# One list transfer per round of the attention loop instead of six

## What is computed

```python
xw = (x @ W).reshape(n_nodes, H, C)
al_s = einsum('nhc,hc->nh', xw, a_src);  al_d = einsum('nhc,hc->nh', xw, a_dst)
logits = leaky_relu(al_s[src] + al_d[dst], 0.2)
m = segment_max(logits, dst)
e = exp(logits - m[dst])
out = segment_sum((e / segment_sum(e, dst)[dst])[:, :, None] * xw[src], dst)
```

## Time and profile before

| what | us |
|---|---|
| median of three runs | 5478.3 |
| span of the profiled execution | 5521.1 |
| loop of layer 0 (from its first gather to its last) | 1356 |
| loop of layer 1 | 1364 |
| loop of layer 2 | 1346 |
| everything else | 1455 |

### The profile page before, as it was taken

The page is one execution under the profiler, slowest core; times in us unless marked ns, Lnnn a source line. Parts: engine busy times, 40 slices in busy tenths (PEclk is TensorE's granted clock), DMA queues, the critical chain, the costliest instruction groups (busy, mean ns, idle before and its releaser), DMA issues. The chain is left out here.

```text
span 5521.1 us, 62679 instructions
## 1 busy us (share of the span) xinstructions
PE 2641.6 (48%) x13804; PEld 1929.0 (35%) x13804; DVE 2377.2 (43%) x7341; ACT 594.6 (11%) x1968; POOL 2781.1 (50%) x2942
## 2 busy tenths in 40 slices
PE   1666774354444555557444554545543333333334
PEld 1555543123333333335233333333433323323323
DVE  5888513334444444442444444444423333333333
ACT  2222300110000000003000000000020000000001
POOL 2000011366666666663566666666446666666663
PEclk9766877667777767768677767677765555555555
DMA  2222564133333333341333333333313222222222
GB/s 61 106 106 96 233 217 157 26 86 89 88 91 88 90 88 91 88 87 44 80 90 89 88 89 92 88 90 90 69 33 46 46 47 46 46 47 46 47 45 22
DMA packets 246608, 451.11 MB, mean 82 GB/s; under 512 B 163452, under 2 KB 165314, under 8 KB 241709
## 3 DMA queue, kind: packets, MB, share of 16 engines
q0 software_dynamic: 122928, 318.15, 24.3%
q1 hardware_dynamic: 111150, 128.71, 6.9%
q10 hardware_dynamic: 12384, 2.25, 0.2%
HBM read 392.07 MB, written 57.21 MB: 81 GB/s over the span
## 5 line engine op out<-in xcount | busy, mean ns | idle before, releaser
L495 POOL DMA_INDIRECT rows_all<-gat_tab,ell x2664 | 2517.1, 945 | 1556.7 <-issue 786.4
L1003 PE MATMUL banks<-rows_all,ident 128*128 128x264 f32 (+1 forms) x5328 | 1823.2, 512 | 2249.2 <-PEq L119 1822.4
L1003 PEld LDWEIGHTS banks<-rows_all,ident 128*128 128x128 f32 x5328 | 1321.6, 289 | 2750.7 <-issue 2557.8
L1599 DVE TENSOR_TENSOR rows_all<-rows_all,banks 128x1024 f32<-128x1024 f32 (+1 forms) x666 | 685.6, 1042 | 247.6 <-issue 162.9
L1574 DVE COPY lrel<-m_all 128x8 f32 x666 | 130.5, 196 | 1492.2 <-issue 1197.2
L789 ACT ACTIVATE banks<-ex_in 128x40 f32<-128x40 f32 x666 | 138.3, 208 | 3780.2 <-ACTq L119 2537.1
L1552 DVE TENSOR_TENSOR acc<-acc,banks 128x264 f32 (+1 forms) x675 | 259.7, 385 | 466.4 <-DVEq L119 297.8
L1545 DVE TENSOR_TENSOR acc<-acc,banks 128x264 f32 (+1 forms) x675 | 257.7, 382 | 114.0 <-issue 109.9
L859 PE MATMUL banks<-rows_all 128*128 128x52 bf16 x4992 | 190.7, 204 | 150.2 <-PEq L119 144.6
L859 PEld LDWEIGHTS banks<-rows_all 128*128 128x128 bf16 x4992 | 179.8, 109 | 175.1 <-issue 173.4
L495 POOL DMA_INDIRECT edges<-sw_d,edge_pick x28 | 32.3, 1154 | 411.4 <-POOLq L119 399.3
(11 more groups left out here) (275 smaller groups left out, 1979.8 us busy)
## 6 DMA issues: line engine op xcount, KB each, us to landing
rows_all<-gat_tab,ell POOLq DMA_INDIRECT x2664
x_t<-adj_d SPq DMA_DIRECT2D x11, 3328.0 KB
y_t<-adj_d SPq DMA_DIRECT2D x11, 3328.0 KB
adj_d<-x_t SPq DMA_DIRECT2D x7, 3328.0 KB, 10.2
adj_d<-y_t SPq DMA_DIRECT2D x6, 3328.0 KB, 10.0
ell<-ell_d SPq DMA_DIRECT2D x666, 2.5 KB
acc<-key_d SPq DMA_DIRECT2D x1, 1664.0 KB, 6.4
acc<-vec_d SPq DMA_DIRECT2D x1, 1664.0 KB
```

Source lines behind the costliest of these rows:

```text
L495: return g.indirect_dma_start(out=dst, out_offset=None, in_=table, in_offset=bass.IndirectOffsetOnAxis(ap=idx, axis=0))
L1003: last = t.matmul(sum_ps[u % SUMS][:, 0:width], ident[:, :], rows[u][:, r * width:(r + 1) * width], start=(r == 0), stop=(r == SLOTS - 1))
L1599: v.tensor_tensor(msg, msg, exp_ps[u][:, 0:SLOTS, :].unsqueeze(3).to_broadcast([P, SLOTS, HEADS, c]), ALU.mult)\
```

## The change

The six list buffers become one buffer `ell_list` of 6 x 5 integers per partition; `ell[u]` is now a slice of it. SP makes one load of 15 KB per round instead of six of 2.5 KB, and there is one semaphore `ell_landed`. POOL takes it, and raises `tile_known`, only ahead of chunk 0. DVE takes `tile_known` only for chunk 0, and gives back `ell_free` only in `weigh(5)`. At the start DVE gives one token of `ell_free` instead of six. The tokens of `rows_free`, the gathers and all arithmetic stay.

```diff
+LISTED = 6
+LISTS = RING // LISTED
-        ell = [sb(f"ell{u}", [P, CHUNK], I32) for u in range(RING)]
+        ell_list = [sb(f"ell_list{n}", [P, LISTED * CHUNK], I32) for n in range(LISTS)]
+        ell = [ell_list[u // LISTED][:, u % LISTED * CHUNK:(u % LISTED + 1) * CHUNK] for u in range(RING)]
-        ell_landed = [sem(f"ell_landed{u}") for u in range(RING)]
+        ell_landed = [sem(f"ell_landed{n}") for n in range(LISTS)]
-                    for u in range(RING):
+                    for n in range(LISTS):
                         take(sp, ell_free)
-                        sp.dma_start(ell[u][:, :], ell_d[:, bass.ds(it * RING + u, 1), :].rearrange("p k c -> p (k c)"))\
-                          .then_inc(ell_landed[u], 16)
+                        sp.dma_start(ell_list[n][:, :], ell_d[:, bass.ds(it * RING + n * LISTED, LISTED), :].rearrange("p k c -> p (k c)"))\
+                          .then_inc(ell_landed[n], 16)
                     for u in range(RING):
-                        take(pool, ell_landed[u], 16)
-                        pool.sem_inc(tile_known, 1)
+                        if u % LISTED == 0:
+                            take(pool, ell_landed[u // LISTED], 16)
+                            pool.sem_inc(tile_known, 1)
                         take(pool, rows_free)
             for u in range(RING):
+                signal(rows_free)
+            for n in range(LISTS):
                 signal(ell_free)
-                signal(rows_free)
                 def known_tile(u):
-                    take(dve, tile_known)
+                    if u % LISTED == 0:
+                        take(dve, tile_known)
                     return chunk_tile(u)
                         signal(exp_in)
-                        signal(ell_free)
+                        if u % LISTED == LISTED - 1:
+                            signal(ell_free)
```

## The result

The changed kernel takes 6039.3 us (median of four runs, 6035.8 to 6050.3) against 5480.4 us for the kernel before (5467.6 to 5487.2): a ratio of 1.102, with a 95% interval of 1.100 to 1.104. It is slower by 10.2%, or 559 us. The profiled execution has a span of 6035.7 us. The experiments are numbered 1 to 12 in the order in which they were run, and "kernel 5" is the kernel of experiment 5.

The account below looks back on a forecast made before the run. Bound: POOL's 24 gathers, 30.0 us of a 36.6 us round, plus 6.6 of pauses. Rounds of 45.3, 45.3 and 45.6 us, with 86 and 23, sum to 5012 against 4066: +946, so 6467, scaled to 6410 us; range 5850 to 6750.

Parts of the forecast that it names:

- the list's cover: SP's list loads: each chunk's list was asked for some 17 us before POOL wants it, hiding the load's latency.
- the turn: Between rounds: last gather's landing 3.0, weigh(5) to its signal 1.9, list load 2.4, POOL restart 0.8; 8.1 us.
- the stall: Sequencers of DVE, PE and ACT stall together after POOL issues gathers back to back, until POOL pauses.
- Step 1: SP's loads: five of six a round removed, with their signals and waits on DVE and POOL; worth 0.
- Step 2: Round's end: POOL waits until weigh(5) frees the list and it is loaded again; 8.1 us, 6.6 to 9.4.
- Step 3: POOL runs 24 gathers unbroken, so the stall comes in every round and stays to the end; rounds 45.3 and 45.6 us.
- Its pace of 11.9 us a chunk: Chunks inside the stall: mean of 6.6 and 17.1 us, so 24 us let chunks 1 and 2 through.
- the stall's onset: Start of the stall in POOL's run: after 8 to 15 gathers, 10 to 17 us into a round; 10 taken.
- rival A: Rounds: the stall comes but weighs less or more, two to four chunks left; total 6060 to 6750, chance 0.77.
- rival D: Rounds: longer pause, later stall, costing one chunk; 38 to 42 us a round, 5640 to 6060, chance 0.09.
- The step from one chunk to the next behind the stall: DVE on the chunks left after the stall: 3.2 us each in layers 0 and 1, 2.7 in layer 2.
- The signs named for the trace: POOL: one 14 to 17 us pause, 24-gather runs; DVE: chunk 0 at once, two long chunks, three quick; busy times unchanged.

Follow-up runs that it names:

- kernel 5: Changed kernel plus a POOL wait before chunk 3's gathers until DVE has weighed chunk 2; 5995.7 us, ratio 1.103.
- kernel 4: Changed kernel with LISTED = 3: two list loads a round into two buffers, three chunks each; 5447.3 us, ratio 0.9937.
- kernel 8: Changed kernel with its one load staged: POOL copies each chunk's list to its own buffer and waits, six copies a round; 5358.2 us, ratio 0.9865.
- kernel 1: Changed kernel plus five 2.5 KB loads a round into spare buffers that nobody reads; 6106.1 us, ratio 1.114.
- kernel 2: Changed kernel plus, in five chunks a round, a DVE signal, an SP wait and four SP semaphore changes, no transfer; 6107.2 us, ratio 1.114.
- kernel 9: Staged single-load kernel with two waited POOL copies a round, three chunks' lists each, instead of six; 5713.7 us, ratio 1.051.
- kernel 11: Staged single-load kernel with six POOL copies issued one chunk ahead, only the first pair waited for; 5527.1 us, ratio 1.017.
- kernel 6: Changed kernel with three of each chunk's four TensorE matmuls left out, so another output; 5835.6 us, ratio 1.074.
- kernel 7: Changed kernel with LISTED = 2: three list loads a round into three buffers, two chunks each; 5418.7 us, ratio 0.9972.
- kernel 10: Staged single-load kernel with three waited POOL copies a round, two chunks' lists each, instead of six; 5503.4 us, ratio 1.013.
- kernel 12: Kernel before plus a spare POOL copy and wait ahead of each chunk; 5259.4 us, ratio 1.105, on a chip where the kernel before takes 4762.0.

## Why the prediction was right, and which terms were off

The verdict was right, and for its reason: the list's cover is gone, POOL stands still at the turn of each round, and the stall comes in the long run of gathers. Kernel 5 shows the turn without the stall, and kernels 4 and 8 that a round with fewer loads costs nothing once the list is given back early. The size was forecast too large, +946 us on the profiled span where +515 came.

- Step 1, the removed loads worth 0: right for the transfers, kernels 1 and 2 differ by 1 us with and without the five. The instructions that go with them are not quite 0: put back into the changed kernel they cost 1.1%.
- Step 2, the turn of 8.1 us (6.6 to 9.4): 7.7 measured, 7.2 in layer 2 (kernel 5). The end of it, list load and POOL's restart, was put at 3.2 us and is 2.8 from chunk 5's exponential to the next gather (1940.91 to 1943.72 in the round shown). The load itself lands in 1.7 us, less than the 2.4 taken: `ell_list<-ell_d` in the profile's list of DMA issues. The Trainium skill ("DMA: Bandwidth & Descriptors", Anatomy of one DMA) gives some 2.0 us of fixed cost, in a section on the DMAs that GpSimd issues. This load is SP's, and the trace has it a little below.
- Step 3, the stall in every round: right, and so was its end (34.0 forecast, some 33 us here, DVE's last long record). Its pace of 11.9 us a chunk can't be checked: the stall holds DVE for 8 to 9 us, and the only chunk in it, chunk 4, is done 2 to 3 us behind its end in layers 0 and 1 (1.7 to its signal was the forecast).
- The step that was off is the stall's onset: 10 us, with 8 to 15 gathers as its span, where for DVE 22 to 25 us and 19 to 20 gathers came. So chunks 1 to 3 passed at DVE's own pace, and two (4 and 5) were left at the end instead of three: 41.9, 42.5 and 39.4 us a round, where 45.3, 45.3 and 45.6 were forecast. Two chunks left is the lower end of rival A, priced at 42.1 us a round and 6060 us, and 6039 were measured; what differs from A is that the onset is later still than its 15 gathers. For SP the 10 us of the forecast were right (9.2 us in kernel 2), but SP has nothing to do then in the changed kernel. The rows for the onset came from first rounds, after pauses of other lengths. What I passed over is what rival D says: the pause before the run is longer and the stall comes later (DVE's onsets in the kernel before, kernels 9 and 11 and the changed one point the same way). I gave D 0.09, against a time of 38 to 42 us a round that two layers touch and one meets. It was against D that layer 0's stall came after 15 gathers behind a long wait; one case of a first round was taken for the rule.
- The step from one chunk to the next behind the stall was 3.2 us in layers 0 and 1 and measured 4.1 and 4.4, with PE at its lower clock (kernel 6). So one chunk fewer took less off the round than 3.2 us.
- Layer 2: I gave it the longest round and it has the shortest. There that step is 2.5 us (2.7 forecast), since TensorE's sums of half width are made in time.
- The stall was said to hold DVE, PE and ACT. Long records are DVE's and SP's. Of ACT's records in the loops none is over 0.5 us, in the kernel before and in the changed one, and PE has none that would tell: that these two do nothing in the stretch is shown, that their sequencers are slow is not.
- The signs named for the trace came, apart from one: one pause a round before chunk 0 (9.8 to 12.8 us, under the 14 to 17), runs of 24, nearly unchanged busy times; but DVE shows four chunks in step and one long one, not one and two.

The rule of batching small transfers from the Trainium skill ("Perfetto Trace Analysis", DMA Optimizations) brought little here: with and without the 79,920 packets the time is the same (kernels 1 and 2), and where the cover stays, three or two loads a round in place of six give 0.3% and 0.6% (kernels 7 and 4). No queue was near full.

Still open: what the stall is. It holds the sequencers of DVE and SP to 0.7 us an instruction while POOL issues gathers, and it depends on POOL's recent pauses, a little on the number of sequencer instructions and, it seems, on the chip. Loading of program code by DMA is not it: in the three loops of the changed kernel the two instruction queues moved 10 packets, and the stall came in each of the 111 rounds. No run here shows the resource behind it.

## What to carry to other kernels

A load that is shared by a whole round has to be given back before the round's last consumer, or its latency lands on the path once a round: take two buffers or more, or copy out of a staging buffer, before counting transfers saved. When an engine's idle time sits where the profile writes "issue", find out what the others do then: a single transfer with the busy engine paced (0.77 us every four gathers, -1.35%) did better here than saved transfers without it (-0.6% at best). Pacing alone was tried only on a chip where the kernel before seems to have no stall, and there it cost 10.5%, so measure on more than one. And a stretch read from the first round of a loop is a poor measure for its steady rounds, where the pauses before it are others.

## What the runs showed of the hardware

- A long run of POOL's indirect gathers, 1.25 us apart, goes with 0.70 us an instruction in DVE's sequencer (median, 26 to 32 us into a round of the changed kernel) in place of 0.05, from the 19th gather or so behind a pause of 9.8 to 12.8 us, and until 4 to 5 us after the last gather's start. SP's sequencer is slow in the same way from 9.2 us on behind the same pauses, while DVE's is not yet (kernel 2).
- Pauses keep it away if they are frequent or long enough: 0.77 us every 4 gathers (kernel 8) or 4.65 and 6.7 us in turn every 12 (kernel 5), but not 0.77 every 8 or 12 (kernels 10 and 9) or 3.65 every 12 (the kernel before).
- Chips differ: on one the kernel before runs 13% faster (4762 against 5480 us), as if it had no stall there, which no trace of it confirms. Gathers there land in 2.6 us (median, kernel 12), against 3.0 and 3.0 in kernel 8, which has the same pauses.
- After 12.57 us without work TensorE does eight matmuls of 264 columns in 3.86 us at a granted clock of 0.50, and the next eight in 2.02 us at 1.00.
- A copy of 128x5 integers on POOL with a wait for it costs 0.77 us between two gathers, though it is busy for 0.20 (kernel 8).
